# A causal attention and feed-forward block: the mask of the row maxima moves from TensorE's products into VectorE's reduction

## What is computed

```python
x = x + layernorm(attention(layernorm(x)))   # 16 heads of 16, rotary positions, causal
x = x + layernorm(ffn(layernorm(x)))         # low rank 64, 1024 hidden, gelu

scores = jnp.einsum('bhid,bhjd->bhij', q, k) * scale
causal = jnp.triu(jnp.ones((n, n), dtype=bool), k=1)
scores = jnp.where(causal, -jnp.inf, scores)
attn = jax.nn.softmax(scores, axis=-1)
out = jnp.einsum('bhij,bhjd->bhid', attn, v)
```

## Time and profile before

| | us |
|---|---|
| median of 3 runs | 1340.21 |
| lowest, highest | 1338.93, 1342.71 |
| span of the profiled execution, first to last instruction | 1352.9 |

### The profile page before, as it was taken

The page is one execution under the profiler, slowest core; times in us unless marked ns, Lnnn a source line. Parts: engine busy times, 40 slices in busy tenths (PEclk is TensorE's granted clock), DMA queues, the critical chain, the costliest instruction groups (busy, mean ns, idle before and its releaser), DMA issues.

```text
span 1352.9 us, 29140 instructions
## 1 busy us (share of the span) xinstructions
PE 1251.7 (93%) x11889; PEld 618.4 (46%) x11889; DVE 935.4 (69%) x1449; ACT 911.8 (67%) x1257; POOL 659.1 (49%) x724
## 2 busy tenths in 40 slices
PE   6789999999999899989999999999999999999994
PEld 2344444544444444544444444444444554445452
DVE  4676776668766876667567767786776687666755
ACT  4326676677667667756767776777576668868784
POOL 4154412882288228812585249524842224426556
PEclk9669999999999999978999999999998899999997
DMA  6643563376626644645456455544474443501412
GB/s 198 162 105 60 119 90 60 84 167 90 119 84 136 109 62 129 127 97 90 70 125 155 68 103 135 149 79 89 117 137 76 80 84 104 159 19 63 156 56 101
DMA packets 99465, 142.43 MB, mean 105 GB/s; under 512 B 25222, under 2 KB 61188, under 8 KB 99332
## 3 DMA queue, kind: packets, MB, share of 16 engines
q1 hardware_dynamic: 99332, 140.58, 47.9%
HBM read 79.70 MB, written 51.38 MB: 97 GB/s over the span
## 4 chain that ended last, share of the span: by engine, by line
PE 73%; ACT 9%; DVE 6%; POOL 3%; DMA 3%; issue 3%; SPq 2%; ACTq 0%; POOLq 0%
PE PV L780 18%; PE RING L762 12%; PE RING L724 12%; PE MI L688 8%; ACT PB L1077 6%; PE MI L790 4%; PE RING L731 4%; PE MI L698 4%; PE RING L824 3%; PE RING L831 3%; DVE MB L899 3%; DVE M L899 2%; PE RING L803 1%; DMA head_sums<-OT 1%; PE MI L679 1%
## 5 line engine op out<-in xcount | busy, mean ns | idle before, releaser
L1077 ACT ACTIVATE PB<-RING 128x1024 f32<-128x1024 f32 (+2 forms) x640 | 582.9, 938 | 262.6 <-PE RING L762 245.4
L899 DVE TENSOR_REDUCE MB<-RING 128x2 f32<-128x1024 f32 (+2 forms) x448 | 502.1, 1145 | 190.7 <-PE RING L724 95.6
L1155 POOL TENSOR_SCALAR_AFFINE_SELECT PB<-PB 128x512 f32<-128x512 f32 x256 | 161.6, 637 | 431.9 <-ACT PB L1077 431.6
L724 PE MATMUL RING<-QK 48*128 48x512 f32 (+3 forms) x1536 | 286.6, 406 | 33.3 <-ACT PB L1077 15.9
L762 PE MATMUL RING<-QK 50*128 50x512 f32 (+3 forms) x1536 | 278.0, 406 | 23.0 <-ACT PB L1077 12.0
L899 DVE TENSOR_REDUCE M<-RING 128x2 f32<-128x768 f32 (+1 forms) x186 | 190.6, 1044 | 89.1 <-PE RING L731 88.2
L780 PE MATMUL PV<-PB,VL 128*32 128x512 f32 (+3 forms) x2048 | 234.8, 536 | 2.2 <-ACT OT L1083 1.4
L724 PEld LDWEIGHTS RING<-QK 48*128 48x128 f32 x1536 | 142.3, 193 | 199.9 <-ACT PB L1077 87.5
L762 PEld LDWEIGHTS RING<-QK 50*128 50x128 f32 x1536 | 134.7, 190 | 185.7 <-ACT PB L1077 72.7
L731 PEld LDWEIGHTS RING<-MASKK,MASKQ 64*128 64x128 f32 x1536 | 144.2, 199 | 8.1
L731 PE MATMUL RING<-MASKK,MASKQ 64*128 64x64 f32 (+1 forms) x1536 | 130.8, 249 | 0.0
(11 more groups left out here) (121 smaller groups left out, 1257.7 us busy)
## 6 DMA issues: line engine op xcount, KB each, us to landing
QK<-split_parts SPq DMA_DIRECT2D x372, 128.0 KB, 5.9
split_parts<-PARTS SPq DMA_DIRECT2D x60, 256.0 KB, 3.1
split_parts<-EO SPq DMA_DIRECT2D x60, 256.0 KB, 3.4
ATT<-OT SPq DMA_DIRECT2D x128, 64.0 KB
INV<-inverse_sums SPq DMA_DIRECT2D x32, 256.0 KB
block_mid<-Y SPq DMA_DIRECT2D x16, 512.0 KB, 3.6
F_X<-block_mid SPq DMA_DIRECT2D x16, 512.0 KB, 5.2
out<-F_Y SPq DMA_DIRECT2D x32, 256.0 KB, 2.1
```

What stands on the lines that cost most here:

```text
L724: ins = e.matmul(m[:, h, i, :], QK[g % 3][r, 0, k, 128 * t:128 * t + 128], QK[g % 3][r, 1, k, k0:k0 + n], start=(i == 0), stop=not open_en ...
L899: e.tensor_reduce(acc, ring(("max", g, s, u), pairs, n), AX.X, ALU.max).then_inc(v_max, 1)
L1077: e.activation(buf[:, :, pairs[0]:pairs[-1] + 1, :], ring(("score", g, s, u), pairs, n), ACT.Exp).then_inc(a_exp, 1)
L1155: e.affine_select(buf[:, :, 0:128], buf[:, :, 0:128], pattern=[[0, 4], [1, 128]], base=0, channel_multiplier=-1, compare_op=ALU.is_ge, fil ...
```

## The change

The four mask products behind each open unit go, with MASKQ, MASKK, ROW, their transfers, fills and casts, and the wait for them. A table TRI (128 x 512, zeros and in its last 128 columns the mask) is loaded once. On VectorE the reduction of an open unit becomes a loop over heads and pairs, each with one instruction that adds the table to the scores, writes the sum back in place into PSUM and takes the maximum along the row. The other 8 units of a group keep their single reduction. v_max now counts an open unit twice, once for each head (`counts_by_head`), and the waits use these counts. `SPLIT_MAX` and `SPLIT_EXP`, which would split the other reductions and the exponentials, are False.

RING has 7 banks now, and MI is its bank 0. The letters m and s replace ABC and abc, and a string of digits, BANKS_TAKEN, names the banks of every step; read out, orders and banks are those of before, step for step. In the feed-forward part the first uses of banks wait for the step before them by the same rule (`FEED`). The two additions of the bias behind the output projection (L923, L924) become one instruction of 512 columns.

```diff
@@ TensorE, a unit of maxima @@
-                                           QK[g % 3][r, 1, k, k0:k0 + n], start=(i == 0), stop=not open_end(g, s))
-                    if open_end(g, s):
-                        w.wait_ge(v_mask, 1)
-                        for z in range(2):
-                            for h in range(2):
-                                r = slice(64 * h, 64 * h + 64)
-                                ins = e.matmul(m[:, h, :, n - 128 + 64 * z:n - 64 + 64 * z], MASKQ[r, z, :],
-                                               MASKK[r, z, :].unsqueeze(1).to_broadcast([64, len(pairs), 64]),
-                                               start=False, stop=(z == 1))
+                                           QK[g % 3][r, 1, k, k0:k0 + n], start=True, stop=True)
                     ins.then_inc(p_max, 1)
@@ VectorE, max_out @@
-                    e.tensor_reduce(acc, ring(("max", g, s, u), pairs, n), AX.X, ALU.max).then_inc(v_max, 1)
+                    found = ring(("max", g, s, u), pairs, n)
+                    if open_end(g, s):
+
+                        w.wait_ge(s_mask, 16)
+                        for h in range(2):
+                            for i in range(len(pairs)):
+                                scores = found[:, h, i, :]
+                                ins = e.tensor_tensor_reduce(out=scores, in0=scores, in1=TRI[:, 512 - n:512], scale=1.0, scalar=-3.0e38,
+                                                             op0=ALU.add, op1=ALU.max, accum_out=acc[:, h, i].unsqueeze(1))
+                            ins.then_inc(v_max, 1)
+                    else:
+                        for heads in (slice(0, 1), slice(1, 2)) if by_head(step) else (slice(0, 2),):
+                            e.tensor_reduce(acc[:, heads], found[:, heads], AX.X, ALU.max).then_inc(v_max, 1)
@@ VectorE, proj_out @@
-                    e.tensor_tensor(YS[c][:, q0, :], MI[:, 0:256], BP[:, :], ALU.add)
-                    e.tensor_tensor(YS[c][:, q0 + 1, :], MI[:, 256:512], BP[:, :], ALU.add).then_inc(o_mi["proj"], 1)
+                    e.tensor_tensor(YS[c][:, q0:q0 + 2, :], BANKS[BANK["proj", b, c, q0][0]].rearrange("p (q d) -> p q d", q=2),
+                                    BP[:, :].unsqueeze(1).to_broadcast([128, 2, D]), ALU.add).then_inc(o_mi["proj"], 1)
@@ who frees a bank @@
+def by_head(step):
+
+    what, g, s, u = step
+    if what == "max_out":
+        return open_end(g, s) or (SPLIT_MAX and reach(g, s)[3] > 256)
+    return SPLIT_EXP and width(s)[3] > 256
...
             def free(step):
                 for before in AFTER[step]:
-                    w.wait_ge(*out_of(before))
+                    w.wait_ge(*out_of(*before))
```

More of the change, by code:

```diff
@@ L29 @@
 ROWS, SHIFT = 48, 50
+SPLIT_MAX, SPLIT_EXP = False, False
 def width(s):
@@ L209, in order_of_work, with counts_by_head @@
         left = {name: iter([step for step in steps if taken_by(engine, step)]) for name, steps in names.items()}
-        order[engine] = []
-        for letter in letters:
-            place = "ABCabc".find(letter) if engine == "PE" else -1
-            step = next(left[("max", "score")[place // 3] if place >= 0 else LETTERS[engine][letter]])
-            order[engine].append(step)
-            if place >= 0:
-                bank[step] = 2 * (place % 3) + 1, 2 * (place % 3) + 2
-            elif step[0] in FIRST_BANKS and step[1] == 0:
-                bank[step] = (int(FIRST_BANKS[step[0]][names[step[0]].index(step)]),)
-            elif step[0] in TAKEN and engine == "PE":
-                bank[step] = (0,)
-            elif step == ("f_turn", 0, 0):
-                bank[step] = 5, 6
-    for step in order["PE"]:
-        if step in bank:
-            after[step] = list(dict.fromkeys(had[i] for i in bank[step] if i in had))
-            had.update(dict.fromkeys(bank[step], step))
-    return order, bank, after
+        order[engine] = [next(left[LETTERS[engine][letter]]) for letter in letters]
+    digits = iter(BANKS_TAKEN)
+    for step in order["PE"]:
+        if step in FEED:
+            bank[step] = FEED[step]
+        elif step[0] in EMPTIES.values():
+            bank[step] = tuple(int(next(digits)) for _ in range(2 if step[0] in ("max", "score") else 1))
+        else:
+            continue
+        after[step] = list(dict.fromkeys(had[i] for i in bank[step] if i in had))
+        had.update((i, (step, h)) for h, i in enumerate(bank[step]))
+    return order, bank, after
+def by_head(step):
[3 more added lines that the diff above has]
+    return SPLIT_EXP and width(s)[3] > 256
+def counts_by_head(steps, what):
+    found, n = {}, 0
+    for step in steps:
+        if step[0] == what:
+            parts = 2 if by_head(step) else 1
+            for h in range(2):
+                found[step[1:] + (h,)] = n + min(h + 1, parts)
+            n += parts
+    return found
 def block_kernel(nc, x, w_qkv, b_qk, b_v, w_proj, b_proj, u1, v1, b1, u2, v2, b2,
@@ L371, in block_kernel @@
         s_spread = sem("s_spread")
-        v_half, v_one, v_pv0, v_bvw, v_mask = (sem(f"v_{n}") for n in ("half", "row", "pv_zero", "bias_wide", "mask"))
+        v_half, v_pv0, v_bvw = (sem(f"v_{n}") for n in ("half", "pv_zero", "bias_wide"))
         a_cst = sem("a_consts")
@@ L450, in ring, with last_of @@
         def ring(step, pairs, n):
-            first = BANK[step][0] - 1
-            return RING[:, first:first + 2, 0:len(pairs) * n].rearrange("p h (k n) -> p h k n", n=n)
-        SCORED = [sum(len(units(width(i)[3])) for i in range(s + 1)) for s in range(SLOTS)]
+            i, j = BANK[step]
+            return RING[:, i:j + 1:j - i, 0:len(pairs) * n].rearrange("p h (k n) -> p h k n", n=n)
+        def last_of(g, s, n):
+            return g, s, len(units(n)) - 1, 1
         SELECTS = [sum(diagonal(i) for i in range(s + 1)) for s in range(SLOTS)]
@@ L840, in tensor @@
                     w.wait_ge(f_y, 2 * (NTH[step] - 1))
+                    if step in FEED:
+                        free(step)
                     for j in range(2):
@@ L1076, in scalar @@
                     w.wait_ge(p_pv, SLOTS * g + s - 3)
-                    e.activation(buf[:, :, pairs[0]:pairs[-1] + 1, :], ring(("score", g, s, u), pairs, n), ACT.Exp).then_inc(a_exp, 1)
+                    scores = ring(("score", g, s, u), pairs, n)
+                    for heads in (slice(0, 1), slice(1, 2)) if by_head(step) else (slice(0, 2),):
+                        e.activation(buf[:, heads, pairs[0]:pairs[-1] + 1, :], scores[:, heads, :, :], ACT.Exp).then_inc(a_exp, 1)
                 elif what == "ot_copy":
```

134 lines of the change are left out of this document (75 added, 59 removed).

## The result

| | before | with the change |
|---|---|---|
| median, us | 1341.46 | 1378.28 |
| lowest to highest | 1338.93 to 1351.63 | 1371.50 to 1379.94 |
| runs | 4 | 4 |
| profiled execution: time, span | not given, 1352.9 | 1376.74, 1375.0 |

The ratio is 1.0229, with an interval of 1.0156 to 1.0301: slower by 2.3%, some 31 us (the medians are 37 apart), where +12 (1352 us) was forecast.

A forecast was written before the change was run, and what follows sets the result against it. TensorE was taken as the bound, but not alone: it waits on PSUM banks shared with VectorE and ScalarE. Removed mask products gave -50 us and VectorE's added work +62, so +12 on the 1340.2 us median: 1352 us, range 1300 to 1410.

The forecast's parts named there:

- the waits for L930: Sign: TensorE's waits for VectorE's maxima of masked units were to rise above 150 us.
- VectorE's busy time: Sign: VectorE's total busy time was to rise by 100 to 130 us.
- the new instruction: Sign: VectorE's add-and-maximum was to take 272 to 290 ns for 128 columns, about 690 for 512, its companion adding 0.07 us.
- TensorE's busy time: Sign: without the mask products, TensorE's busy time was to fall by some 85 us or more.
- new stretches of 0.50 in the granted clock: Sign of being wrong: TensorE newly granted only 1.2 GHz, half its full clock, for stretches of the kernel.
- the gain of 50 us: Attention on TensorE: removing 1536 mask products saves their 3.7% of the wait chain; bounds near 0 to 84 us.
- The loss of 62 us: VectorE's maxima in attention: 1664 more instructions at 0.07 us add 116 us, of which 53% reaches the path.
- The third that was added to 39% by choice: Share of VectorE's growth reaching the path: 39% of reductions already waited for, raised by a third to 53%.
- VectorE's idle time swallows the growth: Rival, chance 0.34: VectorE's 30% idle time in attention absorbs most added work, so faster, 1308 or 1302 us.
- The pair does not overlap: Rival, chance 0.13: the companion waits for its partner on VectorE, growth 280 us, time 1438 us.
- half rate in place: Rival, chance 0.04: reading and writing one PSUM bank doubles VectorE's element cost, 341 us more; 1472 to about 1600 us.
- The clock: Rival, chance 0.09: a less dense TensorE falls to 1.2 GHz three times more often, +30 us, 1382 us.

The follow-up runs named there:

- no_mask: The changed kernel without any mask on the maxima, one plain reduction per unit on VectorE: 1312.63 us, 0.9732 of before; repeated, 1315.23 us, 0.9755.
- plain_pairs: The change without the mask, open units reduced plainly per head and pair, each reduction followed by one over two SBUF elements: 1394.16 us, 1.0374 of before.
- narrow_free: The change with the 128 open units of 128 or 256 columns left unmasked, the 256 wider ones masked on VectorE: 1341.83 us, 0.9949 of before.
- plain_split: The change without the mask, open units reduced by head and pair with plain reductions, 1024 in place of 384: 1328.35 us, 0.9851 of before.
- both: The kernel before with all its mask products, open units reduced as in the change but adding a table of zeros: 1432.02 us, no ratio given.
- before_split: The kernel before, mask products kept, open units reduced by head and pair with plain reductions, 640 more instructions: 1359.34 us, 1.0129 of before.

## Why the prediction was right, and where not

**The sign and the mechanism held.** TensorE lost its mask products, VectorE's growth came back through the banks and outweighed them. In its own form, gain and loss on the path, the measured sum is -36 (`no_mask`) + 62 (1378.28 and 1373.46 less 1312.63 and 1315.23, mean 62) = +26 between kernels of different batches, 29 to 37 by the medians set side by side (1373.46 - 1344.57, 1378.28 - 1341.46), and 21 to 31 by the ratios. Forecast: -50 + 62 = +12. Of the signs that the prediction named, the waits for L930 came (206 us, over 150 expected), but VectorE's busy time rose by 82 us, not by 100 to 130, the new instruction took 325 ns for 128 columns, not 272 to 290, and TensorE's busy time fell by 29.6, not by 85. And one sign of being wrong did appear: new stretches of 0.50 in the granted clock. How far the loss came through the banks alone is therefore less sure than the sign; see the clock below.

**The step that failed is the gain of 50 us.** It was the share of the mask products in the chain, 0.037 x 1352.9. Taking them away, with nothing put in their place, gave 36 of the 84 us that they hold the queue, small savings included. A chain shows what lay on it, not what is left when that goes: TensorE came earlier and waited 25 us longer for the maxima (175 for 150). The text had named this ("only waits longer for ScalarE or VectorE") as the lower bound, and then took the row.

**The loss of 62 us was right by luck: two errors cancel.** VectorE's growth was 91 us, not 116: the pair costs 0.115 us beside its elements, where 0.07 + 0.07 was taken for each pair. Of it 62/91 = 68% reached the time, not 53%; the row that would have given the share, reductions waited for, went to 65%. The third that was added to 39% by choice was too little. It was also wrong to take one share for every dose. By the growth of VectorE's busy time over `no_mask`, 38 us of plain reductions on all open units cost 16 us, 39 on the wide ones 27, the change's 87 cost 62, and the 98 of `plain_pairs` 79; with all the products, 38 cost 15 to 17 and 88 cost 54 or more. The share runs from 0.4 to 0.8. The larger doses paid the larger share, but `narrow_free` at 39 paid as much for each us as the change, so the dose alone does not set it; what does was not separated.

**VectorE's idle time swallows the growth (0.34):** refuted. It worked 75% of the 900 us and TensorE still waited for it 419 times over the kernel. Idle time in the mean gives no slack at a bank that the next product is waiting for. `plain_split` shows how far the idle time goes: a third of its 45 us appears.

**The pair does not overlap (0.13), half rate in place (0.04):** refuted by the timeline, as shown above. The page of the Trainium skill that was weighed (VectorE: DVE Perf Modes, "The TRN2 errata — SBUF-src ops pay a fixed extra latency per instruction") would have put the growth at an estimated 141 us; between neighbours the rows show 91. The forecast's own 116 was nearer, and also too high.

**The clock (0.09): right in size, not in the cause it gave.** Its price was +30 us for three more falls like that of the earlier trace rows, some 80 us at half clock, and its 1382 us was nearer to the 1378.28 and 1373.46 than the forecast. Profiled against profiled it was 187 for 111 us, and at 0.3 to 0.4 us of span each the extra 76 go with 23 to 30 us. It was to come from "a less dense TensorE". That the products are gone is not the reason: `no_mask` lacks them and kept the clock, `both` has them and lost it. That the waits thin TensorE out, and that this lowers the clock, is not excluded. Among kernels without mask products half-clock time tends to rise with the number of waits for maxima: 293 waits with 83 to 122 us (`no_mask`, twice), 362 with 106 to 175 (`narrow_free`), 367 with 90 to 142 (`plain_split`), 419 with 125 to 201 (the change, twice), 423 with 211 to 243 (`plain_pairs`). The order is not clean: 362 waits go with more than 367. With all the products it is 251 waits and 61 to 236 us (about 100 in the middle), 276 and 89 to 137 (`before_split`), 324 and 177 to 289 (`both`). The Trainium skill (TensorE: Matmul & The Clock Gate, "HAM oscillation — how this bites in real kernels") says that idle gaps between bursts bring the half clock back; these rows agree only in that more waits and more half clock mostly go together. The waits here are short, 275 us / 419 = 0.66 us on average in the change, and no run shows that they bring the clock down.

**What stays open.** The three terms can be cut in another way: -37 for the products, +36 for the waits at equal clock, and some 30 us that go with the half clock, most of the slowdown. Whether the waits lower the clock, or a low clock and longer waits have another cause in common, was not separated: no kernel changed the clock and left the waits alone. The waits at equal clock, 36 of 91 us, would be 40% of the growth, close to the 39% with which the prediction began; that is a reading of lines, not a measurement. The same lines put the price at equal clock at 14, 14, 36 and 40 us for 38 (`plain_split`), 39 (`narrow_free`), 87 (the change) and 98 us (`plain_pairs`) of VectorE's growth, 36 to 41% of each: by this estimate the uneven shares lie in the part that goes with the half clock.

## What to carry to other kernels

Where engines hand PSUM banks round a ring, count by how much each unit's banks are held longer against what the other engine saves on that unit: 0.16 against 0.22 us came out level, 0.39 against 0.22 clearly slower, although VectorE was busy less than three quarters of the time. Read what a share of the chain is worth by taking the work away with nothing in its place, and ask at the same time whether it is needed: leaving the mask of the maxima out gave 1312.63 and 1315.23 us, the fastest of all, 2.4 to 2.7% below before. That version is safe only where the masked scores of a diagonal block do not exceed a row's own maximum by so much that its exponentials vanish; within that limit it beats both kernels.

## What the runs showed of the hardware

- The add-and-maximum instruction reads and writes the same PSUM bank at full rate: 0.65 us from one of 512 columns to the next, the read of its accumulator included. That read is 140 ns long but starts together with the next instruction, so that mean durations (719 + 140 ns) overstate the pair.
- A plain reduction of two elements behind one of 512 costs about as much: 0.67 us for both.
- With TensorE 92% busy and 1536 products more than the change, `both` was granted less (0.937 in its fastest run, 0.913 in the profiled one) than a kernel with 10353 products in all (`no_mask`, 91% busy, 0.954 to 0.968). In these kernels the mean share of busy time does not tell the grant; it is itself larger where the clock is low (in the earlier trace rows, 157 products kept TensorE busy for 26.9 of 27.3 us at 0.50, and 243 for 24.2 at 1.00).
- The same kernel, before, took from 1337.48 to 1387.36 us within one batch, and 0.27 us of it (0.38 without one outlying run) went with each us at 1.2 GHz; a profile taken from one such run should be set against its own time and clock.
